# A graph-attention layer with layer norm: the end of each row group moved from VectorE to GpSimd, a comparison moved between two bit operations, scores loaded by head, adjacency in two places instead of four

## The chip, the cores and the metric

The kernel runs on one core of a Trainium2 chip. The metric is the device time of the program in microseconds (us); shown are the median of three runs and one profiled execution. Names of engines: TensorE (PE; its weight loads are PEld), VectorE (DVE), ScalarE (ACT), GpSimd (POOL), SyncE (SP), which issues the transfers here.

## The reference

`x` is 8192 x 128, `adj` is 8192 x 8192 of 0 and 1 as int32 (symmetric, with ones on the diagonal, about 0.2% ones). There are 4 heads of 32 columns.

```
Wh    = (x @ W.T) by head                     # 8192 x 32 for each of 4 heads
e     = leaky_relu(src_i + dst_j, 0.2)        # src, dst: Wh times the two halves of a
e     = -inf where adj[i, j] == 0
alpha = softmax(e over j)
out   = layernorm(x + concat over heads (alpha @ Wh))
```

Since leaky_relu has two slopes, exp(e) is a product of a factor of the row i and one of the column j on either side of the sign of src_i + dst_j. So the kernel needs, for each head, only two 0/1 matrices: `step` (an edge, and the score at or above zero) and `rest` (an edge, and the score below zero). TensorE multiplies them with tables G and F made once from Wh; the row factors alpha and beta are applied to the sums. A column of ones in each table gives the softmax's denominator.

## The kernel before

The 8192 rows are taken in 16 groups of 512 rows (`GROUPS`), each group's 8192 columns in 16 quads of 512 columns (`QUADS`); a quad is 4 blocks of 128 columns by 512 rows. Heads times blocks gives 16 tiles of comparisons a quad. A setup before the loop (some 90 us) makes the projections, the tables `G` (three bf16 parts) and `F` (two fp16 parts), and the scores; group 0 runs from there.

For every quad, the engines do this (lines are those of the profile):

- **SP** issues two transfers of 512 KB of adjacency (L238) into one of `NA` = 4 places of `adj_t`, as soon as the edge operation that last read that place is done (`edge_set`). At quad 6 it also issues the next group's scores `s_all` for all four heads in one transfer of 1024 KB (L228), at quad 4 the store of a finished group (L242) and the load of a group's rows of `x` (L246).
- **POOL** does 5 of the 16 comparisons (L326), then turns the adjacency of two quads ahead into int8 `edge` (L293), for which its transfer must have landed and PE must have transposed the edges that were in that place (`N8` = 2 places). Before the comparisons it waits for `quad_past`, which DVE raises at the end of each quad (L616), so that it is never more than two quads past DVE; and for `rest_done`, since `step` has `NS` = 4 places. In quad 11 it also raises the variance of the group before to the power -0.5 (`rstd`, L297).
- **ACT** does 9 comparisons as a steep sigmoid (L403). After quad 1 it copies the six banks of sums of the group before out of PSUM (`take_sums`, L387), after quad 14 it normalises that group's rows (`normalise`, L393).
- **DVE** does 2 comparisons that take in the edge at once (L522), ANDs the other tiles of `step` with the transposed edges in PSUM (`take_step`, L527 for heads 0 to 2 and L529 for half of head 3), which raises `step_set`, and makes `rest` by XOR and AND (`take_rest`, L539), which raises `rest_set`.
- **PE** multiplies `step` with `G` (64 matmuls, L685), waits for `rest_set`, transposes the edges of two quads ahead (L672), and multiplies `rest` with `F` (64 matmuls, L685), which raises `rest_done`. Around a group it opens and closes the banks (L696, L700).

The order of the work on each engine is the order in which the code is written. The end of a group is the generator `finish` on DVE: behind the quads 1 to 8 of the next group it does, one piece a quad, L562 and L563, L566 and L567, L570, L573 (the parts of the sums added and weighed by alpha and beta), L576 and L579 (reciprocal of the denominator), L583 (times it), L588 (plus x), L592 (row statistics); then L597 and L601 (variance) and, two quads on, L606 (shift). For the last group all of it stands behind the loop. On DVE and ACT the groups 1 to 14 are a loop over pairs of groups, on PE and POOL everything is written out.

Of the kernel before, what the change touches and what calls it, by code (L numbers as in the profile page):

```python
# [6 lines left out]
def gat_layernorm(nc, x, adj, W, a, out):  # L7
# [33 lines left out]

    NA = 4
    N8 = 2
# [25 lines left out]
    with ctx:  # L69
        def sb(name, shape, dt):  # L70
            return ctx.enter_context(nc.sbuf_tensor(name, shape, dt))
# [7 lines left out]
        s_all = sb("s_all", [P, 2, HEADS, ROWS], fp32)  # L79
        adj_t = sb("adj_t", [P, NA, IB, ROWS], i32)  # L80
        edge = sb("edge", [P, N8, IB, ROWS], i8)
# [94 lines left out]
        act_compared = sem("act_compared")  # L176
        quad_past = sem("quad_past")
        pool_compared = sem("pool_compared")
        step_set = sem("step_set")
        rest_set = sem("rest_set")  # L180
# [3 lines left out]
        res_loaded = sem("res_loaded")  # L184
        var_set = sem("var_set")
        rstd_set = sem("rstd_set")
        shift_set = sem("shift_set")
# [22 lines left out]

        SCALED = 14

        def done(n):
            return n + LEAD

        @block.sync
        def _(sync):
# [7 lines left out]

            def load_s(g, n):
                src = sT_v[g].unsqueeze(0).to_broadcast([P, HEADS, ROWS])
                sync.dma_start(s_all[:, n], src).then_inc(s_loaded[n], 16)  # L228

            def load_adj(g, q):  # L230

                k = quad_no(g, q)
                if k < NA:
                    sync.wait_ge(xT_psum, (k + 1) * XT // NA)
# [13 lines left out]
            for g in range(GROUPS):  # L248
                for q in range(QUADS):
                    load_adj(g, q)  # L250
                    if g == 0 and q + 1 == NA:
                        for n in range(2):
                            sync.wait_ge(s_copied, n + 1)
                            sync.dma_start(sT_rows[n], s_rows[:, n]).then_inc(s_stored, 16)
                        sync.wait_ge(s_stored, 32)
                        load_s(0, 0)
# [17 lines left out]
        def _(pool):  # L274
# [13 lines left out]
            def take_edges(k):  # L288
# [4 lines left out]
                nc.gpsimd.tensor_scalar(edge[:, k % N8], adj_t[:, k % NA], 1.0, -1.0, ALU.min, ALU.max).then_inc(edge_set, 1)  # L293

            def inverse_deviation(g):
                pool.wait_ge(var_set, done(g + 1))
                nc.gpsimd.tensor_tensor(rstd[:, :], mv[:, :, 1], half_t[:, :], ALU.pow).then_inc(rstd_set, 1)  # L297
# [16 lines left out]
            for g in range(GROUPS):  # L314
                if POOL_TILES:
                    pool.wait_ge(s_loaded[g % 2], 16 * (g // 2 + 1))
                for q in range(QUADS):
                    k = quad_no(g, q)

                    if k > 1:  # L320
                        pool.wait_ge(quad_past, k - 1)
                    if POOL_TILES:
# [6 lines left out]
                    if k + N8 < GROUPS * QUADS:  # L329
                        take_edges(k + N8)  # L330
                    if q == 11 and g > 0:
                        inverse_deviation(g - 1)
            inverse_deviation(GROUPS - 1)

        @block.scalar
        def _(act):
# [60 lines left out]
            def group(g, n, first=False):  # L397
                act.wait_ge(s_loaded[n], 8 * (g + 2 - n))
                for q in range(QUADS):
# [23 lines left out]
        def _(dve):  # L423
# [90 lines left out]

            def take_step(g, q, n):

                nth = at(dve, quad_no(g, q) + 1)
                if q == 0:
                    dve.wait_ge(s_loaded[n], 8 * (g + 2 - n))
                dve.wait_ge(transposed, nth)  # L520
                for b, h in DVE_TILES:
                    nc.vector.scalar_tensor_tensor(step_u8[:, q % NS, h, b // E, :, b % E], s_all[:, n, h],  # L522
                                                   d_neg[:, q * IB + b, h:h + 1], edgeT8[q % 2][:, b // E, :, b % E],
                                                   ALU.is_ge, ALU.logical_and)
                dve.wait_ge(act_compared, nth)
                dve.wait_ge(pool_compared, nth)
                nc.vector.scalar_tensor_tensor(step[:, q % NS, 0:HEADS - 1], edgeT[q % 2][:, 0:HEADS - 1], ONES,  # L527
                                               step[:, q % NS, 0:HEADS - 1], ALU.bitwise_and, ALU.bitwise_and)
                nc.vector.scalar_tensor_tensor(step[:, q % NS, HEADS - 1, 0:WORDS // U], edgeT[q % 2][:, HEADS - 1, 0:WORDS // U],  # L529
                                               ONES, step[:, q % NS, HEADS - 1, 0:WORDS // U], ALU.bitwise_and, ALU.bitwise_and  # L530
                                               ).then_inc(step_set, 1)

# [8 lines left out]

            CHAIN0, CHAIN_STEP = links[0], 10

            def finish(g):
# [9 lines left out]

                rows = bass.ds(g * IB, IB)

                def per_row(v, width):
                    return v.rearrange("p b h -> p (b h)").unsqueeze(2).to_broadcast([P, CHUNKS, width])

                top, low = acc_sb[:, :, 0:HC], acc_sb[:, :, BC:BC + HC]  # L560
                dve.wait_ge(acc_act, done((g + 2) * BANKS))
                nc.vector.tensor_tensor(low, low, acc_sb[:, :, BC + HC:CH], ALU.add)  # L562
                then(nc.vector.tensor_tensor(top, top, acc_sb[:, :, HC:2 * HC], ALU.add))  # L563
                yield
                wait_last()
                nc.vector.tensor_tensor(low, low, per_row(beta[:, rows, :], HC), ALU.mult)  # L566
                then(nc.vector.tensor_tensor(top, top, acc_sb[:, :, 2 * HC:BC], ALU.add))  # L567
                yield
                wait_last()
                then(nc.vector.tensor_tensor(top, top, per_row(alpha[:, rows, :], HC), ALU.mult))  # L570
                yield
                wait_last()
                then(nc.vector.tensor_tensor(top, top, low, ALU.add))  # L573
                yield
                wait_last()
# [3 lines left out]
                then(nc.vector.reciprocal(rden[:, :, :], rden[:, :, :]))  # L579
                yield  # L580
                wait_last()
                dve.wait_ge(stored, 16 * done(g))
                then(nc.vector.tensor_tensor(y.rearrange("p b (h c) -> p (b h) c", h=HEADS), top[:, :, 0:D_OUT],  # L583
                                             per_row(rden[:, :, :], D_OUT), ALU.mult))
                yield
                wait_last()
                dve.wait_ge(res_loaded, 16 * g + 16)
                then(nc.vector.tensor_tensor(y, y, res, ALU.add))  # L588
                yield
                wait_last()  # L590
                for b in range(IB):
# [9 lines left out]
                nc.vector.tensor_scalar(mv[:, :, 1], mv[:, :, 1], EPS, None, ALU.add).then_inc(var_set, 1)  # L601
                for _ in range(2):
                    yield
                assert got[0] == CHAIN_STEP
                dve.wait_ge(rstd_set, g + 1)
# [3 lines left out]
            def group(g, n, first=False, last=False):  # L609
                closing = iter(()) if first else finish(g - 1)  # L610
                for q in range(QUADS):
                    take_step(g, q, n)
                    take_rest(g, q, waits=not first or q >= NL)
                    if q > 0:
                        next(closing, None)
                    dve.sem_inc(quad_past, 1)  # L616
                for _ in closing:
                    pass

            group(0, 0, first=True)  # L620
            with dve.Fori(0, GROUPS // 2 - 1) as u:
# [122 lines left out]
```

## Time and profile before

| | before |
|---|---|
| median of 3 runs | 1690.55 us (1688.36 to 1693.2) |
| the profiled execution's own time | 1688.86 us |
| span in its profile | 1686.8 us |
| mean granted TensorE clock | 0.962 |
| DVE busy | 1636.8 us (97%) |
| ACT busy | 1529.5 us (91%) |
| PE busy | 1439.9 us (85%) |
| POOL busy | 1435.6 us (85%) |

The page gives for each engine the time in which it had an instruction under way, as a sum over the whole program. Neighbouring instructions of an engine overlap a little, so a duration is somewhat more than the distance from one start to the next; where the text counts a cadence, it takes starts. Idle time is put down to the event that ended it; "issue" means that the profile shows none.

### The profile page before, as it was taken

The page shows a single profiled execution, that of the slowest core. Times are in us where ns is not written, and L with a number is a line of the kernel's source. Part 1 is how long each engine was busy: PE and PEld are TensorE (multiplying, and loading weights), DVE is VectorE, ACT ScalarE, POOL GpSimd, SP SyncE. Part 2 cuts the span into 40 slices and gives each one's busy share as a digit, 9 for nine tenths or more (in the row PEclk, how much of TensorE's full clock was granted, in tenths as well). Part 3 has the DMA queues.
Part 4 walks back from the last instruction along what each step waited for, and adds up shares of the span by engine and source line. Part 5 has one row for each costly group of instructions (what it writes and reads, how often), then busy time and mean ns, then how long its engine had stood idle before and what let it go on. Part 6 is the DMA issues. An engine that isn't in the chain of part 4 may idle for free.

```text
span 1686.8 us, 79434 instructions
## 1 busy us (share of the span) xinstructions
PE 1439.9 (85%) x35205; PEld 1412.5 (84%) x35205; DVE 1636.8 (97%) x1804; ACT 1529.5 (91%) x2556; POOL 1435.6 (85%) x1589
## 2 busy tenths in 40 slices
PE   6069988998888989888898988899888898988986
PEld 6069988998888888888898888898888888888886
DVE  7989999999999999999999999999999999999997
ACT  3699999989989999999989999998999999899994
POOL 1689989897988989898898988889899898989983
PEclk9589999999999999999999999999999999999998
DMA  6266657566565656657466564755557565555630
GB/s 204 75 177 200 202 163 220 175 199 185 162 207 174 197 179 192 203 172 215 157 201 186 189 193 164 215 177 194 174 177 217 169 221 175 192 179 177 193 123 21
DMA packets 161833, 303.31 MB, mean 180 GB/s; under 512 B 9528, under 2 KB 22200, under 8 KB 161464
## 3 DMA queue, kind: packets, MB, share of 16 engines
q1 hardware_dynamic: 161464, 298.03, 56.5%
q8 instruction: 276, 4.52, 1.1%
q14 instruction: 93, 0.76, 0.1%
HBM read 293.67 MB, written 4.33 MB: 177 GB/s over the span
## 4 chain that ended last, share of the span: by engine, by line
DVE 40%; issue 29%; PE 20%; POOL 9%; DVEq 1%; ACT 1%; DMA 0%; SPq 0%; POOLq 0%; ACTq 0%
PE bank L685 17%; DVE step L527 16%; DVE step L522 12%; POOL step L326 6%; DVE step L529 3%; POOL edge L293 2%; PE bank L672 2%; POOL rstd L297 1%; DVE bank L484 1%; DVE rest L539 1%; DVE stats L592 1%; DVE late L573 1%; DVE xr L588 1%; DVE xr L583 1%; DVE G L445 1%
## 5 line engine op out<-in xcount | busy, mean ns | idle before, releaser
L403 ACT ACTIVATE step<-s_all,sd 128x512 uint8<-128x512 f32 x2304 | 1423.2, 719 | 46.1 <-PE bank L685 45.9
L326 POOL TENSOR_SCALAR step<-s_all,sd 128x512 uint8<-128x512 f32 x1280 | 916.8, 734 | 110.8 <-DVEq L616 110.2
L685 PE MATMUL bank<-G,step 128*128 128x99 bf16 x16384 | 789.2, 209 | 132.1 <-DVE step L529 98.4
L685 PEld LDWEIGHTS bank<-G,step 128*128 128x128 fp8e4 x16384 | 750.7, 98 | 155.9 <-DVE step L529 121.3
L539 DVE SCALAR_TENSOR_TENSOR rest<-step,bank 128x2048 int32<-128x2048 int32 x256 | 585.6, 2288 | 10.1
L685 PE MATMUL bank<-F,rest 128*128 128x66 f16 x16384 | 558.2, 195 | 20.8 <-issue 20.7
L685 PEld LDWEIGHTS bank<-F,rest 128*128 128x128 fp8e4 x16384 | 538.5, 98 | 22.2 <-issue 22.2
L293 POOL TENSOR_SCALAR edge<-adj_t 128x2048 int8<-128x2048 int32 x256 | 484.2, 1891 | 82.9 <-PE bank L672 61.0
L527 DVE SCALAR_TENSOR_TENSOR step<-bank,step 128x1536 int32<-128x1536 int32 x256 | 447.7, 1749 | 5.8 <-ACT step L403 5.8
L522 DVE SCALAR_TENSOR_TENSOR step<-s_all,sd,bank 128x512 uint8<-128x512 f32 x512 | 358.9, 743 | 11.4 <-issue 6.1
L672 PE MATMUL bank<-identb,edge 128*128 128x128 bf16 x2048 | 158.7, 221 | 10.5 <-issue 8.1
L672 PEld LDWEIGHTS bank<-identb,edge 128*128 128x128 bf16 x2048 | 124.6, 99 | 11.3 <-issue 8.5
L529 DVE SCALAR_TENSOR_TENSOR step<-bank,step 128x256 int32<-128x256 int32 x256 | 105.7, 413 | 0.0
L387 ACT COPY late<-bank 128x495 f32<-128x495 f32 x96 | 42.7, 550 | 57.6 <-PE bank L700 57.6
L696 PE MATMUL bank<-zeros,identb 128*128 128x2 bf16 x96 | 16.3, 169 | 59.7 <-DVE step L529 58.9
L696 PEld LDWEIGHTS bank<-zeros,identb 128*128 128x128 bf16 x96 | 9.4, 98 | 60.7 <-issue 52.2
L309 POOL TENSOR_TENSOR G<-late,G 128x396 bf16<-128x396 f32 (+1 forms) x22 | 25.6, 1166 | 21.2 <-ACT G L369 13.4
L297 POOL TENSOR_TENSOR rstd<-mv,half_t 128x4 f32<-128x4 f32 x16 | 16.3, 1018 | 21.7 <-DVE mv L601 21.7
L393 ACT ACTIVATE xr<-xr,shift,rstd 128x128 f32<-128x128 f32 x64 | 26.2, 480 | 9.0 <-DVE shift L606 9.0
L347 ACT COPY late<-bank 128x512 f32<-128x512 f32 x16 | 9.4, 586 | 19.2 <-PE bank L638 19.2
L375 ACT CAST G<-bank 128x396 bf16<-128x396 f32 (+1 forms) x22 | 10.8, 490 | 14.2 <-DVE bank L484 14.1
L484 DVE TENSOR_TENSOR bank<-G,s_all 128x396 f32<-128x396 f32 (+1 forms) x44 | 23.1, 572 | 0.0
(74 smaller groups left out, 320.0 us busy)
## 6 DMA issues: line engine op xcount, KB each, us to landing
adj_t<-in_adj SPq DMA_DIRECT2D x512, 512.0 KB, 4.9
s_all<-sT_scratch SPq DMA_DIRECT2D x16, 1024.0 KB, 10.2
adj_t<-in_x SPq DMA_DIRECT2D x16, 256.0 KB, 5.7
xr<-in_x SPq DMA_DIRECT2D x16, 256.0 KB, 5.6
out<-xr SPq DMA_DIRECT2D x16, 256.0 KB, 5.4
sT_scratch<-late SPq DMA_DIRECT2D x2, 64.0 KB, 1.9
step<-in_L_gnn_W SPq DMA_DIRECT2D x1, 64.0 KB
a_col<-in_L_gnn_a SPq DMA_DIRECT2D x2, 0.5 KB
```

The costliest lines, as they stand in the source:

```text
L293: nc.gpsimd.tensor_scalar(edge[:, k % N8], adj_t[:, k % NA], 1.0, -1.0, ALU.min, ALU.max).then_inc(edge_set, 1)
L297: nc.gpsimd.tensor_tensor(rstd[:, :], mv[:, :, 1], half_t[:, :], ALU.pow).then_inc(rstd_set, 1)
L326: last = nc.gpsimd.tensor_scalar(step_u8[:, k % NS, h, n // E, :, n % E], s_all[:, g % 2, h], STEEP, d_steep[:, q * IB + n, h:h + 1], ALU. ...
L387: nc.scalar.copy(late[:, b * USED:b * USED + n_ch * CH], acc[b][:, 0:n_ch * CH]).then_inc(acc_act, 1)
L403: last = nc.scalar.activation(step_u8[:, q % NS, h, b // E, :, b % E], s_all[:, n, h], ACT.Sigmoid, scale=STEEP, bias=d_steep[:, q * IB + ...
L484: last = nc.vector.tensor_tensor(to[m % NU][:, 0:n], Wh[:, blk], v[:, blk, :].unsqueeze(3).to_broadcast([P, n, HEADS, HC]), ALU.mult)
L522: nc.vector.scalar_tensor_tensor(step_u8[:, q % NS, h, b // E, :, b % E], s_all[:, n, h], d_neg[:, q * IB + b, h:h + 1], edgeT8[q % 2][:, ...
L527: nc.vector.scalar_tensor_tensor(step[:, q % NS, 0:HEADS - 1], edgeT[q % 2][:, 0:HEADS - 1], ONES, step[:, q % NS, 0:HEADS - 1], ALU.bitwi ...
L529: nc.vector.scalar_tensor_tensor(step[:, q % NS, HEADS - 1, 0:WORDS // U], edgeT[q % 2][:, HEADS - 1, 0:WORDS // U], ONES, step[:, q % NS, ...
L539: nc.vector.scalar_tensor_tensor(rest[:, q % NL], step[:, q % NS], ONES, edgeT[q % 2], ALU.bitwise_xor, ALU.bitwise_and).then_inc(rest_set, 1)
L672: last = nc.tensor.transpose(edgeT16[q % 2][:, u, b * P:(b + 1) * P], edge16[:, q % N8, b, u * P:(u + 1) * P], identb[:, :])
L685: last = nc.tensor.matmul(acc[k][:, col:col + width], matrix[:, h, n // E, b * P:(b + 1) * P, n % E], values[:, q * IB + n, h].rearrange(" ...
```

## The change

On POOL: the eight operations on whole groups (six of 128x528, two of 128x512 elements) leave `finish` and become `close(g, part)`, which POOL runs behind its edge operation in the quads 2, 3, 4, 5, 6, 7, 9 and 10 (`CLOSING`), and for the last group behind the loop. The wait for `quad_past` is gone with the semaphore. `inverse_deviation` moves from quad 11 to 13. On DVE: `finish` keeps the reciprocal (quad 8), the statistics (quad 11), the variance (quad 12) and the shift (quad 13); the two comparisons of the next quad stand between the AND and the XOR of this one, and of the two ANDs the short one comes first. On ACT: `normalise` moves from behind quad 14 to behind quad 15. On SP: adjacency goes into two places of `adj_t` (the tile keeps four, since `x` passes through it at the start), and the scores of the next group come in four transfers of 256 KB, at quads 6, 8, 10 and 12.

```diff
-    NA = 4
+    NA, NX_PLACES = 2, 4
...
-        SCALED = 14
+        CLOSING = (2, 3, 4, 5, 6, 7, 9, 10)
+
+        S_QUADS = (6, 8, 10, 12)
+
+        SCALED = 15
...
-            def load_s(g, n):
-                src = sT_v[g].unsqueeze(0).to_broadcast([P, HEADS, ROWS])
-                sync.dma_start(s_all[:, n], src).then_inc(s_loaded[n], 16)
+            def load_s(g, n, h):
+                src = sT_v[g, h:h + 1].unsqueeze(0).to_broadcast([P, 1, ROWS])
+                sync.dma_start(s_all[:, n, h:h + 1], src).then_inc(s_loaded[n], 16)
...
-                    if q == 6 and g + 1 < GROUPS:
+                    if q in S_QUADS and g + 1 < GROUPS:
...
-                        load_s(g + 1, (g + 1) % 2)
+                        load_s(g + 1, (g + 1) % 2, S_QUADS.index(q))
...
+            def close(g, part):
...
+                if part == 0:
+                    pool.wait_ge(acc_act, done((g + 2) * BANKS))
+                    nc.gpsimd.tensor_tensor(low, low, acc_sb[:, :, BC + HC:CH], ALU.add).then_inc(low_set, 1)
+                elif part == 1:
+                    nc.gpsimd.tensor_tensor(top, top, acc_sb[:, :, HC:2 * HC], ALU.add).then_inc(top_set, 1)
+                elif part == 2:
+                    pool.wait_ge(low_set, 2 * g + 1)
+                    nc.gpsimd.tensor_tensor(low, low, per_row(beta[:, rows, :], HC), ALU.mult).then_inc(low_set, 1)
+                elif part == 3:
+                    pool.wait_ge(top_set, 4 * g + 1)
+                    nc.gpsimd.tensor_tensor(top, top, acc_sb[:, :, 2 * HC:BC], ALU.add).then_inc(top_set, 1)
+                elif part == 4:
+                    pool.wait_ge(top_set, 4 * g + 2)
+                    nc.gpsimd.tensor_tensor(top, top, per_row(alpha[:, rows, :], HC), ALU.mult).then_inc(top_set, 1)
+                elif part == 5:
+                    pool.wait_ge(top_set, 4 * g + 3)
+                    pool.wait_ge(low_set, 2 * g + 2)
+                    nc.gpsimd.tensor_tensor(top, top, low, ALU.add).then_inc(top_set, 1)
+                elif part == 6:
+                    pool.wait_ge(rden_set, g + 1)
+                    pool.wait_ge(stored, 16 * done(g))
+                    nc.gpsimd.tensor_tensor(y.rearrange("p b (h c) -> p (b h) c", h=HEADS), top[:, :, 0:D_OUT],
+                                            per_row(rden[:, :, :], D_OUT), ALU.mult).then_inc(sum_set, 1)
+                else:
+                    pool.wait_ge(sum_set, 2 * g + 1)
+                    pool.wait_ge(res_loaded, 16 * g + 16)
+                    nc.gpsimd.tensor_tensor(y, y, res, ALU.add).then_inc(sum_set, 1)
...
-                    if k > 1:
-                        pool.wait_ge(quad_past, k - 1)
...
-                    if q == 11 and g > 0:
+                    if q in CLOSING and g > 0:
+                        close(g - 1, CLOSING.index(q))
+                    if q == 13 and g > 0:
                         inverse_deviation(g - 1)
+            for part in range(len(CLOSING)):
+                close(GROUPS - 1, part)
             inverse_deviation(GROUPS - 1)
...
             def group(g, n, first=False, last=False):
                 closing = iter(()) if first else finish(g - 1)
                 for q in range(QUADS):
-                    take_step(g, q, n)
+                    take_step(g, q)
+                    if q + 1 < QUADS:
+                        compare(g, q + 1, n)
+                    elif not last:
+                        compare(g + 1, 0, 1 - n)
                     take_rest(g, q, waits=not first or q >= NL)
-                    if q > 0:
+                    if q >= 8:
                         next(closing, None)
-                    dve.sem_inc(quad_past, 1)
```

`compare` is the comparison part of the old `take_step`, with a semaphore `dve_compared` that `take_step` now waits for. The order of the instructions is shown at three places of the last group, whose code is written out on both engines; in brackets stands what a row waits for.

DVE, two quads of the last group, before: comparison, AND, AND, XOR, then a piece of `finish` (L562 and L563 are the first two of the eight operations).

```order
543 L522 SCALAR_TENSOR_TENSOR step<-s_all,sd,bank 128x512 [waits transposed]
544 L522 SCALAR_TENSOR_TENSOR step<-s_all,sd,bank 128x512
545 L527 SCALAR_TENSOR_TENSOR step<-bank,step 128x1536 [waits pool_compared,act_compared]
546 L529 SCALAR_TENSOR_TENSOR step<-bank,step 128x256
547 L539 SCALAR_TENSOR_TENSOR rest<-step,bank 128x2048 [waits rest_done,step_set]
548 L562 TENSOR_TENSOR late<-late 128x16x33 [waits acc_act]
549 L563 TENSOR_TENSOR late<-late 128x16x33
```

DVE after the change, in the same group, from quad 10 to 11: L579 are the two ANDs, L567 the next quad's comparisons, L590 the XOR, L616 the row statistics.

```order
562 L579 SCALAR_TENSOR_TENSOR step<-bank,step 128x256 [waits pool_compared,act_compared,dve_compared]
563 L579 SCALAR_TENSOR_TENSOR step<-bank,step 128x1536
564 L567 SCALAR_TENSOR_TENSOR step<-s_all,sd,bank 128x512 [waits transposed]
565 L567 SCALAR_TENSOR_TENSOR step<-s_all,sd,bank 128x512
566 L590 SCALAR_TENSOR_TENSOR rest<-step,bank 128x2048 [waits rest_done,step_set]
567 L616 BN_STATS stats<-xr 128x6 [waits sum_set]
```

The XOR no longer stands right behind the AND whose output it reads, and DVE has no operation on a whole group left.

POOL after the change, the quads 9 to 11 of the last group: L368 are the comparisons, L302 the edges, L333 and L338 the last two of the moved operations.

```order
904 L368 TENSOR_SCALAR step<-s_all,sd 128x512 [waits rest_done]
905 L368 TENSOR_SCALAR step<-s_all,sd 128x512 x4
906 L302 TENSOR_SCALAR edge<-adj_t 128x2048 [waits transposed,adj_loaded0]
907 L338 TENSOR_TENSOR xr<-xr 128x512 [waits res_loaded,sum_set]
908 L368 TENSOR_SCALAR step<-s_all,sd 128x512 [waits rest_done]
909 L368 TENSOR_SCALAR step<-s_all,sd 128x512 x4
910 L302 TENSOR_SCALAR edge<-adj_t 128x2048 [waits transposed,adj_loaded1]
911 L368 TENSOR_SCALAR step<-s_all,sd 128x512 [waits rest_done]
```

The comparisons wait for `rest_done` alone, where before they waited for `rest_done` and `quad_past`, and the next quad's comparisons stand behind the moved operation.

## Rows read from the trace of the kernel before

**Rows 1.** Busy time by stretch: groups 1 to 14 (XOR to XOR)
```profile
core 0: us, PE busy (x) PEld busy (x) DVE busy (x) ACT busy (x) POOL busy (x), PEclk, DMA share, GB/s
183.85:1573.71 1389.86, 1237.53 (x30688) 1213.78 (x30683) 1369.53 (x1401) 1303.12 (x2161) 1235.54 (x1359) 0.98 0.61 189
```

**Rows 2.** Timeline of DVE, a quad without a piece of `finish` (start, duration)
```profile
133.00 2.29 DVE L539 SCALAR_TENSOR_TENSOR rest<-step,bank 128x2048 int32<-128x2048 int32 x1
135.21 1.40 DVE L522 SCALAR_TENSOR_TENSOR step<-s_all,sd,bank 128x512 uint8<-128x512 f32 x2
136.53 1.75 DVE L527 SCALAR_TENSOR_TENSOR step<-bank,step 128x1536 int32<-128x1536 int32 x1
138.19 0.42 DVE L529 SCALAR_TENSOR_TENSOR step<-bank,step 128x256 int32<-128x256 int32 x1
138.64 2.29 DVE L539 SCALAR_TENSOR_TENSOR rest<-step,bank 128x2048 int32<-128x2048 int32 x1
```

**Rows 3.** L570 by itself (ns min/median/max)
```profile
L570 DVE TENSOR_TENSOR late<-late,alpha x16: 707/1072/2232, 206.0 to 1676.3; 128x528 f32<-128x528 f32 x16
```

**Rows 4.** Timeline of DVE around the statistics and the variance
```profile
238.14 0.87 DVE L592 BATCH_NORM_STATS2 stats<-xr 128x6 f32<-128x128 f32 x4
239.24 1.41 DVE L522 SCALAR_TENSOR_TENSOR step<-s_all,sd,bank 128x512 uint8<-128x512 f32 x2 [0.23 <-DVE stats L592]
...
544.35 0.37 DVE L597 BATCH_NORM_AGGREGATE mv<-stats 128x2 f32<-128x6 f32 x4
544.97 1.41 DVE L522 SCALAR_TENSOR_TENSOR step<-s_all,sd,bank 128x512 uint8<-128x512 f32 x2
...
579.96 1.41 DVE L522 SCALAR_TENSOR_TENSOR step<-s_all,sd,bank 128x512 uint8<-128x512 f32 x2 [1.00 <-issue]
```

**Rows 5.** Timeline of POOL from its last addition to a group on
```profile
946.77 1.01 POOL L297 TENSOR_TENSOR rstd<-mv,half_t 128x4 f32<-128x4 f32 x1
947.79 3.37 POOL L326 TENSOR_SCALAR step<-s_all,sd 128x512 uint8<-128x512 f32 x5
951.14 1.89 POOL L293 TENSOR_SCALAR edge<-adj_t 128x2048 int8<-128x2048 int32 x1
953.01 3.37 POOL L326 TENSOR_SCALAR step<-s_all,sd 128x512 uint8<-128x512 f32 x5
```

**Rows 6.** POOL's two-input operations in the setup: timeline, then the short form's group
```profile
45.35 0.91 POOL L309 TENSOR_TENSOR G<-late,G 128x396 bf16<-128x396 f32 x1 [7.67 <-issue]
49.53 1.25 POOL L309 TENSOR_TENSOR G<-late,G 128x396 bf16<-128x396 f32 x1 [1.87 <-ACT G L369]
...
L309 POOL TENSOR_TENSOR G<-late,G 128x132 bf16<-128x132 f32 x1 | 0.4, 426 | 0.0
```

**Rows 7.** Waits, whole span: total us, times, longest
```profile
POOL step L326 <- DVEq L616: 110.2, 80, 3.5
ACT late L387 <- PE bank L700: 57.6, 15, 13.6
```

**Rows 8.** Timeline: the scores' transfer issued, and PE behind it
```profile
482.97 0.37 SPq L228 DMA_DIRECT2D s_all<-sT_scratch  x1
...
495.40 3.36 PE L685 MATMUL bank<-G,step 128*128 128x99 bf16 x39 [5.33 <-issue]
```

**Rows 9.** Transfers, us from issue to landing: of the page, then L238's min/median/max
```profile
adj_t<-in_adj SPq DMA_DIRECT2D x512, 512.0 KB, 4.9
s_all<-sT_scratch SPq DMA_DIRECT2D x16, 1024.0 KB, 10.2
...
DMA to landing us min/median/max: 3.8/4.9/13.7
```

**Rows 10.** Timeline of the end of the program
```profile
1673.56 0.71 DVE L562 TENSOR_TENSOR late<-late 128x528 f32<-128x528 f32 x1 [3.93 <-ACT late L387]
...
1677.98 0.25 DVE L579 RECIPROCAL rden<-rden 128x16 f32<-128x16 f32 x1
...
1679.72 0.87 DVE L592 BATCH_NORM_STATS2 stats<-xr 128x6 f32<-128x128 f32 x4
```

More of the change, by code:

```diff
@@ L185, in gat_layernorm @@
         var_set = sem("var_set")
+        low_set = sem("low_set")
+        top_set = sem("top_set")
+        rden_set = sem("rden_set")
+        sum_set = sem("sum_set")
         rstd_set = sem("rstd_set")
@@ L233, in load_adj @@
                 if k < NA:
-                    sync.wait_ge(xT_psum, (k + 1) * XT // NA)
+                    sync.wait_ge(xT_psum, (k + 1) * XT // NX_PLACES)
                 else:
@@ L255, in _ @@
                         sync.wait_ge(s_stored, 32)
-                        load_s(0, 0)
+                        for h in range(HEADS):
+                            load_s(0, 0, h)
                     if q == 4 and g > 0:
@@ L293, in take_edges, with per_row @@
                 nc.gpsimd.tensor_scalar(edge[:, k % N8], adj_t[:, k % NA], 1.0, -1.0, ALU.min, ALU.max).then_inc(edge_set, 1)
+            def close(g, part):
+                top, low = acc_sb[:, :, 0:HC], acc_sb[:, :, BC:BC + HC]
+                def per_row(v, width):
+                    return v.rearrange("p b h -> p (b h)").unsqueeze(2).to_broadcast([P, CHUNKS, width])
+                rows = slice(g * IB, (g + 1) * IB)
+                if part == 0:
[25 more added lines that the diff above has]
+                    nc.gpsimd.tensor_tensor(y, y, res, ALU.add).then_inc(sum_set, 1)
             def inverse_deviation(g):
@@ L397, in group @@
             def group(g, n, first=False):
[L398 removed]
+                act.wait_ge(s_loaded[n], 8 * HEADS * (g + 2 - n))
                 for q in range(QUADS):
@@ L513, in _, with compare @@
             leave(UNITS - 1)
-            def take_step(g, q, n):
-                nth = at(dve, quad_no(g, q) + 1)
[L518 to L524, printed above, removed]
+            def compare(g, q, n):
+                if q == 0:
+                    dve.wait_ge(s_loaded[n], 8 * HEADS * (g + 2 - n))
+                dve.wait_ge(transposed, at(dve, quad_no(g, q) + 1))
+                for b, h in DVE_TILES:
+                    last = nc.vector.scalar_tensor_tensor(step_u8[:, q % NS, h, b // E, :, b % E], s_all[:, n, h],
+                                                          d_neg[:, q * IB + b, h:h + 1], edgeT8[q % 2][:, b // E, :, b % E],
+                                                          ALU.is_ge, ALU.logical_and)
+                last.then_inc(dve_compared, 1)
@@ L525, in take_step @@
+            def take_step(g, q):
+                nth = at(dve, quad_no(g, q) + 1)
+                dve.wait_ge(dve_compared, nth)
                 dve.wait_ge(act_compared, nth)
                 dve.wait_ge(pool_compared, nth)
[L527 to L531, printed above, removed]
+                for part in ((slice(HEADS - 1, HEADS), slice(0, WORDS // U)), (slice(0, HEADS - 1), slice(0, WORDS))):
+                    last = nc.vector.scalar_tensor_tensor(step[:, q % NS, part[0], part[1]], edgeT[q % 2][:, part[0], part[1]],
+                                                          ONES, step[:, q % NS, part[0], part[1]],
+                                                          ALU.bitwise_and, ALU.bitwise_and)
+                last.then_inc(step_set, 1)
@@ L553, in wait_last @@
                     dve.wait_ge(dve_chain, CHAIN0 + g * CHAIN_STEP + got[0])
[L555 to L575, printed above, removed]
+                top = acc_sb[:, :, 0:HC]
+                dve.wait_ge(top_set, 4 * g + 4)
                 then(nc.vector.tensor_scalar(rden[:, :, :], top[:, :, D_OUT].rearrange("p (b h) -> p b h", h=HEADS),
@@ L578, in finish @@
                 wait_last()
[L579 to L590, printed above, removed]
+                nc.vector.reciprocal(rden[:, :, :], rden[:, :, :]).then_inc(rden_set, 1)
+                for _ in range(3):
+                    yield
+                dve.wait_ge(sum_set, 2 * g + 2)
                 for b in range(IB):
@@ L601, in finish @@
                 nc.vector.tensor_scalar(mv[:, :, 1], mv[:, :, 1], EPS, None, ALU.add).then_inc(var_set, 1)
-                for _ in range(2):
+                assert got[0] == CHAIN_STEP
+                for _ in range(1):
                     yield
-                assert got[0] == CHAIN_STEP
                 dve.wait_ge(rstd_set, g + 1)
```

9 lines of the change are left out of this document (5 added, 4 removed).

## The prediction

> **What bounds the kernel now.** I read the busy times by stretch first [rows 1]. The stretch runs from the first XOR of group 1 to the first XOR of group 15, 14 groups in 1389.86 us, so a group takes 99.28 us. The reader should see that DVE is busy for 1369.53 us of it, 97.8 us a group, ACT for 93.1, PE for 88.4 and POOL for 88.3. Then I read DVE's own row of instructions [rows 2]: from XOR to XOR it is 5.64 us (133.00 to 138.64) with no gap, so 16 quads cost 90.2 us and the rest of the 99.28, which is 9.1 us, is the end of the group before, laid between quads. DVE sets the pace. The waits [rows 7] confirm it from the other side: POOL waits 110.2 us for the semaphore that DVE raises at the end of a quad, and ACT 57.6 us for the banks at the groups' ends.
>
> Two more things stand in the trace. L570, an operation with two inputs in SBUF, takes 707 ns at best, 1072 in the median, 2232 at most [rows 3]; POOL's comparisons run beside it. And once in most groups PE stands still for "issue" right behind the scores' transfer: that is issued at 482.97, and PE goes on at 495.40 after 5.33 us of idleness for which no semaphore is named [rows 8], while transfers of adjacency, 4.9 us in the median, take up to 13.7 [rows 9].
>
> **DVE after the change.** It loses eight operations a group. It keeps the statistics, 1.10 us from start to next start, the variance, 0.62, both from [rows 4], the reciprocal (0.25 by itself [rows 10]; with the short maximum ahead of it I take 0.4), the shift (0.1) and half of the 1.00 us at the loop's branch [rows 4], which comes once in two groups: 2.7 us together. So 6.4 us a group go (9.1 less 2.7), disturbances among them.
>
> The new order gives a little more. From start to next start, 2048 elements take 2.21 us (L539) and 1536 take 1.66 (L527) [rows 2], 1.07 ns an element, which would make 0.29 for the 256 of L529. It takes 0.45, and the XOR behind it reads what it wrote. Now comparisons stand between them. Of the 0.16 I take 0.10 a quad, since the fixed part of an instruction is in doubt, with 0 as the other end. DVE's own need is then 16 x 5.54 + 2.7 = 91.3 us a group (92.9 if the gap stays).
>
> **POOL after the change.** Its cadence where nothing holds it is 947.79 to 953.01, which is 5.22 us a quad [rows 5], so 83.5 a group; the power adds 1.0 [rows 5]. The eight operations are bounded by two rows of the setup [rows 6]: alone, 396 elements take 0.91 us, and 132 take 0.426; the slope of 1.83 ns an element (and a fixed part of 0.18 us) gives 0.91 + 132 x 0.00183 = 1.15 us for 528. The upper end is the usual 1.25 us for 396, beside DVE work with two SBUF inputs, scaled in full: 1.67. I take 1.20, near the lower end, since DVE keeps almost no such operation and the second input is now f32 rather than bf16; less 0.04 of overlap between neighbours, eight are 9.3 us. POOL's need: 83.5 + 1.0 + 9.3 = 93.8 us. **POOL becomes the engine with the longest row**, by 2.5 us over DVE.
>
> The Trainium skill speaks against such a move: GPSIMD Engine Reference, 3.1 (side-by-side cycle accounting), gives a two-input addition of 2048 f32 elements 4497 ns on GpSimd and 2293 on DVE, and keeps "use DVE for elementwise" as its rule. With a fixed part of 0.18 us such an operation of 528 would be an estimated 1.29 us by that page, and the forecast about 11 us longer; no run here shows f32 with f32 on POOL yet.
>
> Can POOL use all its time? It is tied at two places. It makes the edges for two quads ahead, and may do so only when PE has transposed two quads before, so it can be ahead of DVE's need by some 4 us: the transposes follow the XOR of quad q - 2, the AND of quad q comes two cadences (11.1) after it, and edges, moved operation and comparisons take 6.4 of these. In the six quads with a moved operation from 2 to 7 it takes 5.22 + 1.16 = 6.38 against DVE's 5.54 and loses 0.84 a quad, 5.0 us; before quad 2 it has gained only about 3 (its wait for the variance in quad 13 cuts its lead there to about 1 us: after that wait come the power, 1.0, and comparisons, 3.35, against a quad of 5.6). So DVE waits some 2 to 3 us for `pool_compared` in quads 7 to 11, and POOL 0.6 us for the variance in quad 12 to 13. Either way round: 93.8 + 0.6, or 91.3 + 2.9. I take **94.3 us a group**.
>
> **The other engines.** ACT had 93.1 us of work a group [rows 1], of which the copies (2.7) lie partly beside PE's last matmuls; it has 1.2 us to spare, and its wait of 3.8 us a group (57.6 / 15) [rows 7] is what it loses first. Its normalising, one quad later, waits for the shift in quad 13, still two quads apart; I cost it at nothing, and ACT's lead hides it, or it costs 1 to 2 us if that lead is gone. PE has 88.4 us with its slow stretches and stays below. The rest comes 1.3 us later than before against the AND; PE has its 64 matmuls of G for cover, and a bank opened late costs what it cost before.
>
> **Adjacency in two places** takes the transfers' lead away: a load may be issued when the edges two quads earlier are done, and must have landed two cadences less one edge operation later, 2 x 5.22 - 1.87 = 8.6 us. The second of two transfers lands 0.6 + 4.9 = 5.5 us after the first is issued [rows 9]. So 3 us are left, nothing waits. **Scores by head**: 1024 KB took 10.2 us [rows 9], a quarter takes an estimated 2.6, so a load behind one lands by 8.1: just in time. What goes is the pile of 1024 KB and several loads in front of PE's code, so the 5.33 us hole [rows 8] should shrink or vanish. I count no gain for it beyond POOL's undisturbed cadence.
>
> **The sum**, against the profiled execution (span 1686.8, with 2.1 around it 1688.86; the median lies 1.7 above that). Group 0 gains 0.10 a quad, 1.7 us. Groups 1 to 14: 14 x (99.28 - 94.3) = 69.7. Group 15: 4.9. The end: the eight operations with the reciprocal took 1673.56 to 1679.72, 6.2 us [rows 10]; on POOL, 8 x 1.20 and 0.75 for the reciprocal and two handovers are 10.4, so it loses 4.2. Together 1.7 + 69.7 + 4.9 - 4.2 = 72.1, so the span is 1614.7, the execution 1616.8, the median **1618 us**.
>
> **The rivals.**
> - *POOL's operations are dear.* At 1.67 us they add 8 x 0.47 = 3.8 us a group: 57 us in 15 groups, 4 at the end, so 1679. For it: 20 of the 22 rows of the setup are 1.25, not 0.91. Against: they ran beside DVE operations with two SBUF inputs. Between the ends, each 0.1 us is 12 us of time. Chance 0.16 for over 1648.
> - *POOL isn't the bound after all* (its operations hide, or cost nearer 1.0): DVE at 91.3 to 92.0 gives 2.3 to 3.0 us less a group, 1573 to 1583. Against: the sum of POOL's own row is longer than this. Chance 0.10.
> - *PE's holes stay*: 5.3 us once a group, of which DVE's slack with the new order (the two ANDs, 2.1 us [rows 2], less the transposes themselves, an estimated 0.5) hides 1.6: 3.7 x 15 = 56 us, 1674. The trace speaks against it, since the hole comes behind the large transfer. Chance 0.07.
> - *Two places starve POOL*, the rival on the other side. With two places, two quads of POOL can't be shorter than a pair's landing plus the edge operation: (L + 1.9) / 2. At L = 10.5 us that is 6.2 us a quad, the old 99.3 a group, and with the slower end 1694 in all; at 13.7, the longest single load [rows 9], 7.8 us a quad, 125 a group and 2075 in all. It decides from L = 10.5 on as a mean over all quads; the median is 5.5. Chance 0.05. The Trainium skill (SBUF - State Buffer, "Who interferes with whom") has another reason for a disappointment, DVE operations with two SBUF inputs and GpSimd's reads keeping each other out. [Rows 3] agree, 707 to 2232 ns; after the change such operations are nearly gone from DVE, so by that rule the disturbance goes too.
> - *The change doesn't do what it says* (DVE was held by something else): DVE's row without gaps [rows 1, 2] leaves 0.02, within 10 us of before.
>
> **How the numbers follow.** The forecast's own case has 0.60, within 1600 to 1648 (a price of POOL's operation from 1.05 to 1.45 makes that). On the low side the range goes to 1592, half way to the case below; on the upper side to 1655, which takes in the cheaper half of the dear operations. Outside lie most of the case below, the rest of the dear operations and the holes, some 2 in 10 with the rival of the two places. About 0.3% (5 us) is what a measurement of this kernel can tell from no change: faster 0.93, the same 0.02, slower 0.05.
>
> **What would show it.** In the profile after: DVE busy at about 1530 us, with waits for POOL's comparisons of 2 to 3 us a group in quads 7 to 11; POOL at 93 to 95% busy, its new operations at 1.15 to 1.3 us each; no wait of POOL for DVE's quads, and next to none for adjacency; PE's holes under 2 us; XOR to XOR 5.54 us in quads without waits; the end 4 us longer. I am wrong if POOL's new operations take over 1.45 us, if POOL waits for transfers by more than 1 us a group, or if DVE shows no waits at all.

## The result, and the profile after

The changed kernel takes 1620.36 us (median of 4 runs, 1620.3 to 1621.61) against 1689.45 for the one before; the ratio of the two is 0.9589, 95% interval 0.9572 to 0.9607. The forecast was 1618, in 1592 to 1655. The page's first part:

```profile
span 1618.5 us, 78908 instructions
PE 1428.7 (88%) x35205; PEld 1390.3 (86%) x35205; DVE 1546.3 (96%) x1676; ACT 1523.2 (94%) x2556; POOL 1529.5 (95%) x1717
```

The stretch of groups 1 to 14, again from XOR to XOR, answers to [rows 1]:

```profile
core 0: us, PE busy (x) PEld busy (x) DVE busy (x) ACT busy (x) POOL busy (x), PEclk, DMA share, GB/s
183.60:1507.92 1324.32, 1227.07 (x30662) 1193.03 (x30659) 1292.60 (x1290) 1297.00 (x2161) 1312.18 (x1471) 1.00 0.61 197
```

A group takes 94.59 us (1324.32 / 14), where it took 99.28. POOL is busy for 93.7 of them, before for 88.3; DVE for 92.3, before 97.8. Of the 68.3 us by which the span is shorter, 65.5 lie in this stretch, 2.5 behind it and 0.3 ahead of it.

POOL's timeline in two neighbouring quads of group 10, with the two last of the moved operations, and where it waits:

```profile
1079.63 3.45 POOL L368 TENSOR_SCALAR step<-s_all,sd 128x512 uint8<-128x512 f32 x5
1082.99 1.96 POOL L302 TENSOR_SCALAR edge<-adj_t 128x2048 int8<-128x2048 int32 x1
1085.35 1.06 POOL L333 TENSOR_TENSOR xr<-late,rden 128x512 f32<-128x512 f32 x1 [0.40 <-DVE rden L611]
1086.40 3.39 POOL L368 TENSOR_SCALAR step<-s_all,sd 128x512 uint8<-128x512 f32 x5
1089.75 1.90 POOL L302 TENSOR_SCALAR edge<-adj_t 128x2048 int8<-128x2048 int32 x1
1091.60 1.29 POOL L338 TENSOR_TENSOR xr<-xr 128x512 f32<-128x512 f32 x1
...
1106.67 1.92 POOL L302 TENSOR_SCALAR edge<-adj_t 128x2048 int8<-128x2048 int32 x1
1108.99 1.02 POOL L342 TENSOR_TENSOR rstd<-mv,half_t 128x4 f32<-128x4 f32 x1 [0.40 <-DVE mv L625]
```

The reader should see a row with no gap but two of 0.40 us. The moved operations take 1.06 to 1.40 us in the median. DVE now has the gaps (the waits of the whole span; total, times, longest):

```profile
ACT xr L439 <- DVE shift L630: 35.3, 16, 12.8
DVE step L579 <- POOL step L368: 20.0, 42, 0.9
DVE step L567 <- PE bank L700: 13.5, 25, 1.1
POOL rstd L342 <- DVE mv L625: 7.7, 16, 1.6
POOL xr L333 <- DVE rden L611: 6.6, 16, 0.6
```

The line of [rows 7] in which POOL waited 110.2 us for DVE's quads is gone. PE's holes without a named cause are 1.3 us at most, where [rows 8] had 5.33.

DVE around the reciprocal holds something that was not foreseen:

```profile
1081.31 2.28 DVE L590 SCALAR_TENSOR_TENSOR rest<-step,bank 128x2048 int32<-128x2048 int32 x1
1083.51 1.47 DVE L608 TENSOR_SCALAR rden<-late 128x16 f32<-128x16 f32 x1
1085.01 0.25 DVE L611 RECIPROCAL rden<-rden 128x16 f32<-128x16 f32 x1
1085.18 2.03 DVE L579 SCALAR_TENSOR_TENSOR step<-bank,step 128x256 int32<-128x256 int32 x2
```

L608, the maximum of 16 numbers a partition, takes 1.47 us. It begins in the middle of POOL's edge operation (1082.99 to 1084.95) and ends when that has ended and POOL stands still. Before, the same operation took 0.17, but in all 16 groups it fell into a pause of POOL.

### The profile page after: what moved, and what is told of

It is laid out like the page before. It is cut to its first block, busy times and chain, and to the rows that moved or that the text cites. A ratio compares the mean times of both kernels' runs of the same rounds, so it can differ in the third digit from the quotient of the medians.

```text
span 1618.5 us, 78908 instructions
## 1 busy us (share of the span) xinstructions
PE 1428.7 (88%) x35205; PEld 1390.3 (86%) x35205; DVE 1546.3 (96%) x1676; ACT 1523.2 (94%) x2556; POOL 1529.5 (95%) x1717
## 4 chain that ended last, share of the span: by engine, by line
POOL 63%; DVE 14%; issue 12%; ACT 6%; PE 3%; DVEq 0%; DMA 0%; POOLq 0%; SPq 0%; ACTq 0%
POOL step L368 38%; POOL edge L302 18%; ACT step L449 6%; DVE rest L590 4%; PE bank L713 3%; DVE step L579 3%; DVE step L567 2%; POOL xr L338 1%; POOL late L329 1%; POOL late L314 1%; POOL late L316 1%; POOL late L322 1%; DVE bank L530 1%; DVE stats L616 1%; POOL late L325 1%
## 5 line engine op out<-in xcount | busy, mean ns | idle before, releaser
L368 POOL TENSOR_SCALAR step<-s_all,sd 128x512 uint8<-128x512 f32 x1280 | 875.2, 727 | 0.0
L713 PE MATMUL bank<-G,step 128*128 128x99 bf16 x16384 | 780.6, 207 | 45.7 <-DVE step L579 25.1
L713 PEld LDWEIGHTS bank<-G,step 128*128 128x128 fp8e4 x16384 | 742.1, 97 | 57.8 <-DVE step L579 31.9
L590 DVE SCALAR_TENSOR_TENSOR rest<-step,bank 128x2048 int32<-128x2048 int32 x256 | 582.7, 2276 | 0.0
L579 DVE SCALAR_TENSOR_TENSOR step<-bank,step 128x256 int32<-128x256 int32 (+1 forms) x512 | 532.1, 1079 | 26.8 <-POOL step L368 20.0
L713 PE MATMUL bank<-F,rest 128*128 128x66 f16 x16384 | 549.4, 194 | 6.6 <-issue 6.1
L713 PEld LDWEIGHTS bank<-F,rest 128*128 128x128 fp8e4 x16384 | 529.5, 98 | 8.2 <-issue 7.5
L302 POOL TENSOR_SCALAR edge<-adj_t 128x2048 int8<-128x2048 int32 x256 | 493.0, 1926 | 27.5 <-DMA adj_t<-in_adj 21.2
L567 DVE SCALAR_TENSOR_TENSOR step<-s_all,sd,bank 128x512 uint8<-128x512 f32 x512 | 357.6, 740 | 13.6 <-PE bank L700 13.5
L439 ACT ACTIVATE xr<-xr,shift,rstd 128x128 f32<-128x128 f32 x64 | 26.4, 484 | 35.3 <-DVE shift L630 35.3
L608 DVE TENSOR_SCALAR rden<-late 128x16 f32<-128x16 f32 x16 | 21.3, 1329 | 10.9 <-POOL late L329 10.9
L314 POOL TENSOR_TENSOR late<-late 128x528 f32<-128x528 f32 x16 | 18.7, 1168 | 11.8 <-ACT late L433 11.8
```

The costliest lines, as they stand in the source:

```text
L314: nc.gpsimd.tensor_tensor(low, low, acc_sb[:, :, BC + HC:CH], ALU.add).then_inc(low_set, 1)
L368: last = nc.gpsimd.tensor_scalar(step_u8[:, k % NS, h, n // E, :, n % E], s_all[:, g % 2, h], STEEP, d_steep[:, q * IB + n, h:h + 1], ALU. ...
L439: last = nc.scalar.activation(y[:, b], y[:, b], ACT.Identity, scale=rstd[:, b:b + 1], bias=shift[:, b:b + 1])
L567: last = nc.vector.scalar_tensor_tensor(step_u8[:, q % NS, h, b // E, :, b % E], s_all[:, n, h], d_neg[:, q * IB + b, h:h + 1], edgeT8[q % ...
L579: last = nc.vector.scalar_tensor_tensor(step[:, q % NS, part[0], part[1]], edgeT[q % 2][:, part[0], part[1]], ONES, step[:, q % NS, part[0 ...
L590: nc.vector.scalar_tensor_tensor(rest[:, q % NL], step[:, q % NS], ONES, edgeT[q % 2], ALU.bitwise_xor, ALU.bitwise_and).then_inc(rest_set, 1)
```

## The experiments

Each run was timed beside the kernel before. A difference given in us is one between medians; by the ratios the differences from the changed kernel are up to 2 us smaller or 1 us larger. Four of the runs lie so near the changed kernel that their ratios to before overlap with its own (0.9572 to 0.9607); this is said where it matters.

**1. Which engine sets the pace.** To POOL's row an addition is added, to DVE's six row statistics.

```diff
+                elif part == 6:
+                    pool.wait_ge(top_set, 4 * g + 4)
+                    nc.gpsimd.tensor_tensor(low, low, top, ALU.add).then_inc(low_set, 1)
```

> The changed kernel with one more addition of 128x528 f32 per group on POOL, in quad 8, where none stands; its result goes to a part of the sums that nobody reads. Theory (POOL is the bound, 94.6 us a group): its price, 1.2 to 1.35 us, comes back in full in all 16 groups, +17 to +22 us. Rival (DVE still sets the pace and POOL's row is full only because it follows DVE closely): 0 to +5 us.

```diff
+                if n is not None:
+                    yield
+                    for i in range(6):
+                        last = nc.vector.bn_stats(idle[:, i], s_all[:, n, i % 4, i // 4 * P:(i // 4 + 1) * P])
```

> The changed kernel with six more row statistics of 128x128 on DVE per group (about 1.2 us by the row of 0.28 us each), in quad 14, their result unread. Theory (POOL bound, DVE waits 1.4 us a group for it in quads 5 to 10): the waits take it up, 0 to +4 us. Rival (DVE bound): +17 to +20 us.

Measured: 1637.58 us with the addition on POOL (ratio to before 0.9685, 0.9659 to 0.9710), which is 17.2 more than the changed kernel, 1.08 a group (the addition itself has a median of 1.24, and neighbours on POOL overlap a little; by the ratios it is 16). 1624.17 with 1.2 us a group more on DVE (0.9601, 0.9575 to 0.9627), 3.8 more and within the overlap; DVE's waits for POOL's comparisons fell from 20.0 to 11.7 us. POOL's row sets the pace; what is added to DVE's goes into its waits.

**2. The order on DVE and the wait for its quads.** Each is put back alone.

```diff
-                    take_step(g, q)
-                    if q + 1 < QUADS:
-                        compare(g, q + 1, n)
-                    elif not last:
-                        compare(g + 1, 0, 1 - n)
+                    compare(g, q, n)
+                    take_step(g, q)
```

> The changed kernel with DVE's old order: comparisons, long AND, short AND, XOR. Theory: DVE's cadence goes back from 5.51 to 5.64 us a quad, 2.1 us a group, of which its 1.4 us of waiting hides most, so +0 to +12 us. Rival (the order is what the gain came from, by letting DVE go on while POOL is late): +30 us or more.

```diff
+                    if k > 1:
+                        pool.wait_ge(quad_past, k - 1)
```

> The changed kernel with the wait for DVE's quads back on POOL. Theory: POOL leads DVE by less than 2 us in most quads, so the wait bites only around quads 0 to 3, +0 to +15 us. Rival (the wait was the brake of the kernel before): +40 us or more.

Measured: 1625.49 us (0.9614, 0.9589 to 0.9640) with the old order, 1624.36 (0.9602, 0.9577 to 0.9628) with the wait. Both intervals overlap with that of the changed kernel, so each is worth some 5 us or less here. In the trace the old order's cadence is 5.64 us and the new one's 5.51, so DVE did gain 0.13 us a quad, and POOL's row covers it.

**3. Transfers.** The number of places and the split of the scores are put back, each alone and both together.

```diff
-    NA, NX_PLACES = 2, 4
+    NA, NX_PLACES = 4, 4
```

> The changed kernel with adjacency in four places again, the scores still by head. Theory: two places cost and bring nothing by themselves, since a pair lands in 5.5 us of 8.6: -2 to +5 us. Rival (fewer loads in flight are what keeps PE's code from waiting): +15 us or more, with PE's holes of over 3 us back.

```diff
-        S_QUADS = (6, 8, 10, 12)
+        S_QUADS = (6,)
...
-                src = sT_v[g, h:h + 1].unsqueeze(0).to_broadcast([P, 1, ROWS])
-                sync.dma_start(s_all[:, n, h:h + 1], src).then_inc(s_loaded[n], 16)
+                src = sT_v[g].unsqueeze(0).to_broadcast([P, HEADS, ROWS])
+                sync.dma_start(s_all[:, n], src).then_inc(s_loaded[n], 16)
```

> The changed kernel with the next group's scores in one transfer of 1024 KB at quad 6, adjacency in two places. Theory: the transfer takes 10 us, and the loads of adjacency behind it land too late for two places, so POOL waits for transfers once a group by 3 to 5 us, and PE's hole comes back: +30 to +90 us. Rival (POOL's lead hides it): 0 to +10 us.

> The changed kernel with both undone: four places, scores in one transfer. Theory: POOL doesn't wait for adjacency, but PE's hole of 3 to 5 us is back in most groups and POOL, which has no time to make up, loses what its lead doesn't hide: +10 to +50 us. Rival (the hole stays harmless, as it mostly was before): 0 to +8 us.

| scores | two places | four places |
|---|---|---|
| by head | 1620.36 | 1616.94 |
| in one transfer | 1639.93 | 1664.30 |

The ratios to before are 0.9570 (0.9539 to 0.9602) for four places and scores by head, 0.9704 (0.9671 to 0.9736) for two places and one transfer, 0.9838 (0.9801 to 0.9876) for four places and one transfer. Four places by themselves are as good as two or a little better. The one transfer costs 19.6 us with two places and 47.4 with four. PE and DVE of the last kernel, group 4:

```profile
486.80 0.74 PE L712 MATMUL bank<-G,step 128*128 128x99 bf16 x13
492.24 3.27 PE L712 MATMUL bank<-G,step 128*128 128x99 bf16 x39 [4.70 <-issue]
```

```profile
489.17 2.07 DVE L578 SCALAR_TENSOR_TENSOR step<-bank,step 128x256 int32<-128x256 int32 x2
496.23 1.41 DVE L566 SCALAR_TENSOR_TENSOR step<-s_all,sd,bank 128x512 uint8<-128x512 f32 x2 [4.99 <-PE bank L699]
```

PE stands still for 4.70 us behind the large transfer, the transposes (L699) are late, and DVE waits 4.99 us for them before its comparisons. In all, the waits of this kernel name PE's transposes so:

```profile
DVE step L566 <- PE bank L699: 73.5, 29, 6.5
POOL edge L301 <- PE bank L699: 52.2, 25, 5.3
```

The expectation for two places and one transfer had POOL wait for late loads of adjacency; that was wrong. Its only waits for them are those at the start of the program, as before. The cost is the hole in PE there as well; with two places it is shorter (over 4 us in two groups only, against ten).

What PE lacks in a hole can be read from the packets of this queue, which every page lists among the transfers:

```profile
q8 instruction: 276, 4.52, 1.1%
```

They are packets of 16 KB, in the median 5.4 to 5.6 us apart in these kernels. In the kernel before, one starts at 482.61 and the next only at 493.15; it ends at 494.12, and PE, idle since 490.07, goes on at 495.40. All holes of more than 1.2 us without a named cause, from 150 us on, in the kernel before, the two here and the one with the ends alone of experiment 4 (69 together) end like this, 1.22 to 1.61 us after the end of such a packet. And counted in PE's own instructions (matmuls, weight loads and those of its sequencer), all 69 begin at the same place modulo 256, to within one instruction; 16 KB for 256 instructions is 64 bytes each. So PE stops where a piece of its code ends and the next has not come. Between 150 and 1500 us, two such packets are more than 9 us apart 12 times with four places and one transfer, 3 times with two places and one transfer, and never with the scores by head, with two places or four. That the packet is late because of the transfers in front of it is inferred from this comparison.

**4. One part on the kernel before.** The ends on POOL alone, and the scores by head alone.

> The kernel before with the groups' ends on POOL alone (old order on DVE, POOL paced, four places, one transfer of scores). Theory: the move alone gives most of the gain of 69 us; with the losses of the other parts added (5 for the order, 4 for the pace, 10 to 50 for the scores), 1640 to 1675 us. Rival (the parts work only together): 1685 us or more.

> The kernel before with one part of the change alone: the scores by head, at quads 6, 8, 10 and 12. Theory (the hole cost the kernel before little by itself, but moved POOL against DVE's two-input operations): PE's holes of 3 to 5 us are gone, groups take the 98 us that the undisturbed ones took before, and the time falls by 8 to 20 us. Rival (it is worth as much there as in the changed kernel): -40 us or more.

Measured: 1676.81 us (0.9925, 0.9901 to 0.9950) with the ends on POOL alone, 1672.72 (0.9894, 0.9875 to 0.9912) with the scores by head alone. So the move is worth 13 us by itself, and the scores by head 17; with the small parts the two are worth 69. They need each other: a full row on POOL has no slack for PE's holes, and without the holes the old row on DVE is still 98 us a group. The small parts count for more where the holes are: the kernel with four places and one transfer differs from the one with the ends alone only in DVE's order and the wait for its quads, and is 12.5 us faster (by the ratios 15). The ends on POOL with the scores by head, but with the old order and the wait together, were not run. With the ends alone on POOL, PE's holes go through:

```profile
POOL edge L302 <- PE bank L698: 56.5, 30, 8.5
DVE step L569 <- PE bank L698: 22.3, 15, 6.0
DVE step L580 <- POOL step L370: 19.1, 39, 0.8
```

And with the scores by head alone, POOL keeps its place against DVE's two-input operations. L570 of [rows 3] is L571 here:

```profile
L571 DVE TENSOR_TENSOR late<-late,alpha x16: 707/718/1193, 204.3 to 1660.4; 128x528 f32<-128x528 f32 x16
```

Its median falls from 1072 to 718 ns, and the eight operations together from 108.0 us of DVE's time to 95.8, which is 12.2 of the 17 us. DVE hardly waited for PE before (1.1 us in all), so most of what the holes cost came by way of POOL, which came late and fell upon DVE's operations.

**5. To take POOL's two waits away.** The maximum goes to POOL, and the statistics one quad earlier, so that the variance is there when POOL asks for it.

```diff
+                    nc.gpsimd.tensor_scalar(rden[:, :, :], top[:, :, D_OUT].rearrange("p (b h) -> p b h", h=HEADS),
+                                            TINY, None, ALU.max).then_inc(den_set, 1)
...
-                for _ in range(3):
+                for _ in range(2):
                     yield
```

> The changed kernel with the maximum for the reciprocal on POOL (a 128x16 operation) and the row statistics one quad earlier. Theory: POOL's two waits of 0.4 us a group for DVE go, the small operation costs 0.1: 94.6 less 0.7 a group, -6 to -11 us. Rival (the bound has already passed to ACT or DVE): -3 to +2 us.

Measured: 1691.72 us (1.0014, 0.9994 to 1.0033), 71 us more than the changed kernel and the whole gain gone. The rows that say why, of L625, which adds a constant to 4 numbers a partition:

```profile
L625 DVE TENSOR_SCALAR mv<-mv x16: 170/6286/6294, 250.2 to 1684.3; 128x4 f32<-128x4 f32 x16
```

```profile
1145.62 6.29 DVE L625 TENSOR_SCALAR mv<-mv 128x4 f32<-128x4 f32 x1
1151.82 2.08 DVE L583 SCALAR_TENSOR_TENSOR step<-bank,step 128x256 int32<-128x256 int32 x2
```

```profile
1144.73 1.92 POOL L303 TENSOR_SCALAR edge<-adj_t 128x2048 int8<-128x2048 int32 x1
1146.61 3.42 POOL L372 TENSOR_SCALAR step<-s_all,sd 128x512 uint8<-128x512 f32 x5
1149.96 1.92 POOL L303 TENSOR_SCALAR edge<-adj_t 128x2048 int8<-128x2048 int32 x1
1151.99 1.04 POOL L346 TENSOR_TENSOR rstd<-mv,half_t 128x4 f32<-128x4 f32 x1
```

L625 begins at 1145.62 inside an edge operation and ends at 1151.91, when POOL has run seven instructions without a gap and at last stands still (1151.88), because it waits for L625. In the changed kernel the same operation takes 0.17 us, since it comes while POOL already waits for it. The wait of 0.40 us that I set out to remove was what kept DVE from being shut out for 6. DVE's 6.1 us stand in front of the AND, and PE and POOL wait behind it; it happens in 15 groups, 92 us in all, of which 71 reach the time.

```profile
PE bank L713 <- DVE step L583: 100.8, 38, 6.0
POOL edge L303 <- PE bank L700: 74.6, 47, 4.0
```

The two edits of this run were not timed apart, but the trace clears the other one: the maximum takes POOL 0.27 us, and the reciprocal on DVE 0.24, beside POOL's edge operation.

**6. A better balance.** Built on the last one, with four places and a comparison tile given from POOL to DVE or ACT in two quads, so these two carry its fault.

```diff
+    ACT_MORE, DVE_MORE = (), (3, 5)
+    MOVED = (2, 1)
...
-                        for n, h in POOL_TILES:
+                        for n, h in pool_tiles(q):
```

> As the one with the maximum on POOL and earlier statistics, adjacency in four places, and one comparison tile of POOL done by DVE in quads 3 and 5. Theory: POOL's row falls by 2 x 0.67 to 92.4 us a group, DVE's rises to about the same, ACT's 92.6 is next: 92.7 to 93.5 us a group, 1590 to 1605 us in all. Rival (POOL's and DVE's waits for each other eat it): 1608 us or more.

> The same with the tile done by ACT in quad 7 and by DVE in quad 4. Theory: ACT's row becomes the longest with 93.2 us a group, 1595 to 1608 us in all, 3 to 8 us more than with both on DVE. Rival: ACT's waits take it up, and it is as fast as the other.

Measured: 1677.33 us (0.9913, 0.9886 to 0.9939) with both on DVE and 1674.35 (0.9908, 0.9888 to 0.9927) with one on ACT. The operation that adds the constant has medians of 5743 and 5866 ns in their traces. They are 14 and 17 us faster than the one they were built on, and whether the balance would help the changed kernel stays open: it was not tried without the earlier statistics.

No run beats the changed kernel beyond the interval; with four places it measured 1616.94 against 1620.36, ratios to before 0.9539 to 0.9602 against 0.9572 to 0.9607.

## Why the prediction was right

- *POOL takes DVE's place as the engine that sets the pace.* Right, and shown by experiment 1: 17.2 us for an addition on POOL, at most 3.8 for as much on DVE.
- *The price of the moved operations, 1.20 us.* The eight medians run from 1.06 (L333) to 1.40 (L329), 9.57 us together, so 1.20 each. The spread was not foreseen: the three multiplications are at or below 1.15, L314, L316 and L322 at 1.17 to 1.20, L329 at 1.40 and L338 at 1.29, though all five are additions. Why these two are dearer stays open. The Trainium skill's figure (GPSIMD Engine Reference, 3.1) had led to an estimate of 1.29; the trace has 1.20 in the mean. One reading of the setup was wrong: of its 22 rows 17 are 1.25 and one 1.20, not 20; three are 0.91 and one is the short form.
- *94.3 us a group*: 94.59 measured. The difference is 0.3 x 14 = 4 us, nearly all by which the span missed (1618.5 against 1614.7). POOL's cadence is 5.22, as forecast; its waits were put at 0.6 and are 0.8, and 93.8 and 0.6 are 94.4, where the sum went on with 94.3.
- *DVE's cadence of 5.54*: 5.51, so the gap between the short AND and the XOR had cost 0.13, not 0.10. It made no difference, as forecast.
- *DVE waits 2 to 3 us a group for POOL's comparisons in quads 7 to 11*: 1.4, from 20.0 us in all, in quads 6 to 8 and 11. Another 1.2 us a group went into L608, which I had costed at its old 0.17, and 0.8 into the shift (L630, two inputs in SBUF, 0.92 us in the median for 0.16 before). **This is the step that was wrong in kind**: the text said that with the two-input operations gone from DVE the disturbance goes too. The operations that were left include a one-input form that POOL shuts out as well, and the shift, which has two inputs in SBUF itself. It was harmless only because POOL had the longer row; that the forecast did not suffer from it was luck. The size of what it can do is in experiment 5.
- *ACT costs nothing*: right; it waits 35.3 us in all for the shift, 12.8 of it at the end, and had that to spare.
- *The end, 4.2 us longer*: L314 starts at 1601.55 and the statistics at 1611.46, 9.9 us against 6.2 of [rows 10], so 3.7.
- *Two places starve nothing*: right. A load takes 4.7 us in the median and 10.0 at most. The quarter of the scores was mis-sized: 5.3 us in the median, twice the estimated 2.6, and still nothing waits.
- *The holes go, and no gain is counted for it*: the holes went (1.3 us at most), but the account was too small. I held the hole for nearly harmless and priced its return at 56 us only in a rival, from 5.3 us a group; the fourteen holes before are 1.7 to 5.4 us, 3.8 in the mean. Measured, its return costs 47.4 us in the changed kernel with four places and 19.6 with two. The forecast came out right since it was a sum of rows without holes; had the scores stayed in one transfer, the same sum would have been wrong by that.

## What to carry to other kernels

When work is moved from the engine that sets the pace, build the row of the engine that receives it from undisturbed durations, add it up for a period, and compare it with the others: that sum was within 0.3%. Then ask what used to be absorbed by the slack that is now spent, since the holes in PE cost the kernel 17 us before and 47 after. And before you remove a short wait between two engines that share something, look whether a small operation of the other one gets through in just that pause.

## What the runs showed of the hardware

- A DVE `tensor_scalar` on f32 in SBUF with a handful of elements (128x16, 128x4) can be shut out by GpSimd for several of its instructions: 0.17 us while GpSimd stands still, 1.47 behind one edge operation, 2.24 in the median with DVE's old order, and 6.29 behind seven instructions in a row, with no turn at any of the six handovers between them. It can get a turn at a handover, though: with DVE's old order 4 of 15 took 0.21 to 0.25 us across the passage from one GpSimd comparison to the next, with the ends alone on POOL 6 of 15 took 0.21 to 0.31. What decides it stays open. The Trainium skill (SBUF - State Buffer, "Who interferes with whom") names `tensor_scalar` among the operations that can take the shared pair of ports, if its operands meet further conditions, and says the loser blocks for the whole instruction; the trace shows that it can be several instructions. A reciprocal of the same size took 0.24 us in the run of experiment 5 in 15 groups, each time beside a GpSimd edge operation.
- Behind a 1024 KB transfer of scores PE stopped for 1.7 to 5.4 us in 14 of 15 groups, 7 to 11 us after its issue (issued at 482.97, idle from 490.07 to 495.40 before the change); with four of 256 KB, two quads apart, 1.3 us at most in the changed kernel. PE's code came in packets of 16 KB, one for 256 instructions, and PE went on 1.2 to 1.6 us after the one it lacked had landed.
- Additions of 128x528 f32 on GpSimd took 1.12 to 1.43 us, multiplications with a factor held over 33 elements 1.09 to 1.18.
